# A routed feed-forward block on one core: routing steps of four links, search levels with fewer output tiles, tables loaded later

## The reference, cut to what matters

```python
h = rms_norm(x, gamma)                       # x: 2 x 2048 x 512
light = gelu(h @ w1_l + b1_l) @ w2_l + b2_l  # hidden 256, all tokens
s = einsum('bnd,d->bn', x, routing_token)
b = -relu(s)
for _ in range(50):                          # EPS = 0.1, K = 8
    a = EPS * log(K) - EPS * logsumexp((s + b) / EPS)   # over the 2048 tokens
    b = -relu(s + a)
scores = exp((s + a + b) / EPS)
sel = top_k(scores, 512)                     # per batch row
heavy = gelu(rms_norm(x[sel]) @ w1_h + b1_h) @ w2_h + b2_h   # hidden 2048
out = light; out[sel] += heavy * gain(scores)
```

## Time and profile before

| | us |
|---|---|
| median of 3 runs | 4053.99 (4047.73 to 4062.09) |
| the profiled execution, its own time | 4051.82 |
| its span | 4050.0 |
| PE busy in the span | 3908.2 (96%) |
| DVE busy | 2421.5 (60%) |
| ACT busy | 2004.7 (49%) |

### The profile page before, as it was taken

One profiled execution on the slowest core, in us unless ns is written; L12 is line 12 of the kernel. 1 busy time (PEld: TensorE's weight loads), 2 busy tenths in 40 slices (PEclk: granted clock), 3 DMA queues, 4 the chain that ended last, 5 costly groups with the idle time before them and its releaser, 6 DMA issues. The chain is left out here.

```text
span 4050.0 us, 58949 instructions
## 1 busy us (share of the span) xinstructions
PE 3908.2 (96%) x18715; PEld 2140.9 (53%) x18715; DVE 2421.5 (60%) x3329; ACT 2004.7 (49%) x3355; POOL 2684.8 (66%) x1402
## 2 busy tenths in 40 slices
PE   8999999999999999999999999999979999967899
PEld 7754444444444444444444444444448888854344
DVE  3466666666666666666666666666527777755400
ACT  3335555555555555555555555555434555533010
POOL 1138888888888888888888888888954444410010
PEclk9999999999999999999999999999989999989999
DMA  7632223222232342232222322223222333335510
GB/s 223 170 92 58 58 61 95 71 64 58 61 89 76 84 121 58 64 104 59 63 58 61 97 68 63 59 61 92 70 78 87 104 101 104 99 113 195 197 31 11
DMA packets 393979, 352.22 MB, mean 87 GB/s; under 512 B 192811, under 2 KB 267051, under 8 KB 392872
## 3 DMA queue, kind: packets, MB, share of 16 engines
q1 hardware_dynamic: 325800, 326.02, 28.0%
q10 hardware_dynamic: 66048, 16.78, 1.9%
q0 software_dynamic: 1920, 6.29, 0.5%
HBM read 142.63 MB, written 89.70 MB: 57 GB/s over the span
## 5 line engine op out<-in xcount | busy, mean ns | idle before, releaser
L328 POOL TENSOR_TENSOR acc<-acc,probs 128x1024 f32<-128x1024 f32 x894 | 2127.0, 2379 | 259.9 <-ACT probs L798 134.2
L928 DVE TENSOR_REDUCE maxes<-ps 128x1 f32<-128x1024 f32 x1024 | 1251.0, 1222 | 699.2 <-PE ps L579 694.7
L801 ACT ACTIVATE probs<-ps,far_bias 128x1024 f32<-128x1024 f32 (+7 forms) x1280 | 1021.9, 819 | 1017.2 <-DVE near_s L945 556.3
L614 PE MATMUL ps<-probs,v_head 128*64 128x512 f32 x4096 | 993.4, 606 | 2.0 <-ACT ctx_out L784 1.9
L579 PE MATMUL ps<-stacks 64*128 64x512 f32 x2048 | 748.4, 445 | 16.1 <-issue 7.3
L594 PE MATMUL ps<-stacks 64*128 64x512 f32 x1792 | 660.2, 448 | 0.0
L593 PE MATMUL ps<-stacks 128*128 128x512 f32 x2048 | 617.2, 418 | 1.2 <-ACT probs L798 1.2
L594 PEld LDWEIGHTS ps<-stacks 64*128 64x128 f32 x1792 | 275.9, 184 | 501.3 <-issue 329.4
L614 PEld LDWEIGHTS ps<-probs,v_head 128*64 128x64 f32 x4096 | 248.7, 136 | 483.3 <-issue 481.1
L593 PEld LDWEIGHTS ps<-stacks 128*128 128x128 f32 x2048 | 349.8, 188 | 216.9 <-issue 163.5
L945 DVE TENSOR_TENSOR near_s<-ps,near_bias 128x384 f32<-128x384 f32 (+2 forms) x576 | 284.7, 494 | 264.4 <-PE ps L594 241.4
(11 more groups left out here) (248 smaller groups left out, 4716.6 us busy)
## 6 DMA issues: line engine op xcount, KB each, us to landing
stacks<-c_k SPq DMA_DIRECT2D x128, 256.0 KB, 2.5
stacks<-c_q SPq DMA_DIRECT2D x128, 256.0 KB, 2.6
stacks<-c_d SPq DMA_DIRECT2D x256, 128.0 KB, 2.7
scr_v<-probs ACTq DMA_DIRECT2D x32, 512.0 KB, 4.1
stacks<-c_q SPq DMA_DIRECT2D x128, 128.0 KB, 2.7
v_head<-scr_v SPq DMA_DIRECT2D x32, 512.0 KB, 3.7
scr_ctx<-ctx_out SPq DMA_DIRECT2D x128, 128.0 KB, 2.3
both_ctx<-scr_ctx SPq DMA_DIRECT2D x32, 512.0 KB, 3.9
```

Of the source, the lines that this page charges most:

```text
L328: pool.tensor_tensor(acc[:, qb, :], acc[:, qb, :], pr, ALU.add).then_inc(s["summed"], 1)
L614: mm = pe.matmul(ps[64 * half:64 * half + 64, PV, :], v_head[:, side, kt, :], probs[:, st % PT_RING, half * 512:(half + 1) * 512], start=k ...
L801: ins = act.activation(probs[:, st % PT_RING, a:z], sc[:, a:z], ACT.Exp, bias=bias)
L928: dve.tensor_reduce(maxes[:, qt, pair:pair + 1], ps[:, bank:bank + 2, :], AX.XY, ALU.max).then_inc(s["max_done"], 1)
```

## The change

`hidden_of`: from step 6 on; what is left after step 49 (16 matmuls) is done after the loop. Scores are kept in units of EPS in a layout where partitions 0 to 63 hold batch row 0 and 64 to 127 row 1 (`s_half`, 128 x 2 x 16). A step is: DVE `arg` = min(ahead - log, 0); ACT exponential with the sum over its 32 columns in `sums`; PE sums over each half of the partitions with `own`; ACT logarithm read from PSUM. Beside that DVE keeps `lift` (the sum of the logarithms) and `ahead`. The wide table `s_max` is still used for the final scores and is loaded behind the fourth chunk. The other edits are order: w1, tables and `xb` behind the last chunk, gamma passes behind the GELUs, the row copy on DVE, two light tiles per level instead of four with three PSUM banks instead of four, the tables for the counts behind the search, and the last 12 tiles interleaved with the count matmuls of batch row 1.

```diff
-HIDDEN_FROM, HIDDEN_STEP = 2, 4
+HIDDEN_FROM, HIDDEN_STEP = 6, 4
+SPLIT_AT = 3
-LIGHT_IN_LEVEL = 4
+LIGHT_IN_LEVEL = 2
-LIGHT_IN_STEP = LIGHT_IN_LEVEL * LEVELS
+LIGHT_IN_STEP = LIGHT_IN_LEVEL * (LEVELS + 1)
...
 # SP
-            for b in range(NB):
-                sp.dma_start(s_max[:, b, 0:NT]..., scr["s"]...[b]).then_inc(s["s_in"], 16)
+            for b in range(NB):
+                for half in range(2):
+                    s_in(b, half)
...
-                if ch == 2:
-                    for j in range(4):
-                        xb_in(j)
                 if ch == 3:
-                    for dst, name in LOADS: ...
-                    for dst, name in ROWS: ...
+                    for b in range(NB):
+                        sp.dma_start(s_max[:, b, :]..., scr_s[b]).then_inc(s["s_max_in"], 16)
+            for dst, name in LOADS: ...
+            for j in range(4):
+                xb_in(j)
+            for dst, name in ROWS: ...
+            sp.dma_start(w1[:], io["w1h"]).then_inc(s["w1_in"], 16)
...
 # PE
             def light_mm(j):
-                if j >= 4:
-                    pe.wait_ge(s["light"], j - 3)
+                if j == 0:
+                    pe.wait_ge(s["hidden"], NCHUNK * LM)
+                if j >= 3:
+                    pe.wait_ge(s["light"], j - 2)
-                    mm = pe.matmul(ps[:, 4 + j % 4, :], ...)
+                    mm = pe.matmul(ps[:, 1 + j % 3, :], ...)
             for i in range(N_ITERS):
                 pe.wait_ge(s["ex"], i + 1)
-                pe.matmul(ps[:, 0, 0:NB * NT], ones[:], ex[:]...)
+                pe.matmul(ps[:, 0, 0:1], own[:], sums[:], start=True, stop=True).then_inc(s["mm"], 1)
                 for ch, m, at in hidden_of(i):
                     hidden_mm(ch, m, at)
+            pe.wait_ge(s["neg_a"], 1)
+            pe.matmul(ps[:, 0, 0:NB], ones[:], neg_a[:], start=True, stop=True).then_inc(s["neg_mm"], 1)
+            for ch, m, at in hidden_of(N_ITERS):
+                hidden_mm(ch, m, at)
             pe.wait_ge(s["score"], 1)
...
             mm.then_inc(s["bc"], 1)
+            light_mm(0)
+            light_mm(1)
...
-            for j in LIGHT_LAST:
+            for t, j in enumerate(LIGHT_LAST):
                 light_mm(j)
-            for t in range(NT - HM // 2):
                 hot_mm(1, t)
...
-                    if b == 0 and m < HM // 2:
-                        hot_mm(1, NT - HM // 2 + m)
+                    if b == 0 and m < NT - len(LIGHT_LAST):
+                        hot_mm(1, len(LIGHT_LAST) + m)
...
 # ACT
-                act.activation(ex[:], dif[:], ACT.Exp, scale=1.0 / ROUTE_EPS).then_inc(s["ex"], 1)
-                act.wait_ge(s["total"], i + 1)
-                act.activation(logs[:], total[:], ACT.Ln, scale=1.0 / K_ROUTE).then_inc(s["logs"], 1)
-                if i == 0:
+                act.activation(powers[:], arg[:], ACT.Exp, accum_out=sums[:]).then_inc(s["ex"], 1)
+                act.wait_ge(s["mm"], i + 1)
+                act.wait_ge(s["lift"], i + 1)
+                act.activation(log[:], ps[:, 0, 0:1], ACT.Ln, scale=1.0 / K_ROUTE).then_inc(s["logs"], 1)
+                if i == SPLIT_AT:
...
-            act.copy(rows[:], ps[:, 4:8, :]...).then_inc(s["bcr"], 1)
...
 # DVE
-                dve.tensor_tensor(low[:], s_max[:], neg_a[:]..., ALU.min)
-                dve.tensor_tensor(dif[:], low[:, :, 0:NT], spread(low[:, :, NT]), ALU.subtract)
+                dve.tensor_scalar(arg[:], ahead[:], log[:], 0.0, ALU.subtract, ALU.min).then_inc(s["dif"], 1)
+                if i:
+                    dve.tensor_tensor(lift[:], lift[:], log[:], ALU.add).then_inc(s["lift"], 1)
+                    dve.wait_ge(s["lift"], i + 1)
+                    dve.tensor_scalar(ahead[:], scaled[:], lift[:], None, ALU.subtract).then_inc(s["ahead"], 1)
-                dve.tensor_reduce(total[:], ps[:, 0, 0:NB * NT]...)
-                dve.scalar_tensor_tensor(neg_a[:], logs[:], ROUTE_EPS, low[:, :, NT], ALU.mult, ALU.add)
...
+            dve.tensor_tensor(low[:], s_max[:], spread(ps[:, 0, 0:NB]), ALU.subtract).then_inc(s["kept"], 1)
+            dve.tensor_copy(rows[:], ps[:, 4:8, :]...).then_inc(s["bcr"], 1)
...
-                if lv:
-                    for j in light_of_level(lv - 1):
-                        light_out(j)
+                for j in light_of_level(lv - 1):
+                    light_out(j)
...
+                    if b == 1 and t < len(LIGHT_LAST):
+                        light_out(LIGHT_LAST[t])
```

More of the change, by code:

```diff
@@ L1566 @@
 GAMMA_PIECES = HEAVY // 512
-GAMMA_FROM = 33
+HALF = P // NB
 def routed(nc, io, scr, out, index):
@@ L1588, in routed @@
         above = sb("above", [P, P])
-        s_max = sb("s_max", [P, NB, NT + 1])
-        top, top_row, top_diag = sb("top", [P, NB]), sb("top_row", [NB, 1]), sb("top_diag", [NB, NB])
-        low = sb("low", [P, NB, NT + 1])
+        s_max = sb("s_max", [P, NB, NT])
+        s_half = sb("s_half", [P, 2, NT])
+        scaled, ahead, arg, powers = (sb(n, [P, 2 * NT]) for n in ("scaled", "ahead", "arg", "powers"))
+        sums, log, lift = (sb(n, [P, 1]) for n in ("sums", "log", "lift"))
+        top, top_row, top_wide = sb("top", [P, 1]), sb("top_row", [1, NB]), sb("top_wide", [1, P])
+        low = sb("low", [P, NB, NT])
         dif, ex = sb("dif", [P, NB, NT]), sb("ex", [P, NB, NT])
-        total, logs = sb("total", [P, NB]), sb("logs", [P, NB])
         neg_a = sb("neg_a", [P, NB])
@@ L1623, in routed @@
         ps = c.enter_context(nc.psum_tensor("r_ps", [P, 8, 512], F32))
-        HOT, TURN = 0, 6
-        s = {n: sem(n) for n in """weights const zero s_in top_own top_turned top_row top_diag top_mm top gam low dif ex mm total logs neg_a arg kept sc1 sc score w
+        HOT, TURN, PAIRS = 0, 6, (4, 1)
+        s = {n: sem(n) for n in """weights w1_in const zero s_in s_max_in top_own top_turned top_row top_wide top_mm lift scaled ahead gam dif ex mm logs neg_a neg_mm arg kept sc1 sc score w
             bc bcr t1 cnt en en_mm f1 f2 base over mm1 r1 r2 r3s sel mm2 p1 p2 place hot hot_mm pairs pairs_tr parts4 gain edge_own edge_mm edge picked index
@@ L1632, in routed @@
         block = c.enter_context(nc.Block())
-        LOADS = [(w1, "w1h"), (gamma, "gamma_h"), (b1, "b1h"), (tokens, "tokens"), (steps, "steps"), (above, "above")]
+        LOADS = [(gamma, "gamma_h"), (b1, "b1h"), (tokens, "tokens"), (steps, "steps"), (above, "above")]
         ROWS = [(b2, "b2h"), (places, "places")]
@@ L1649, in _, with s_in @@
         def _(sp):
-            for b in range(NB):
[L1652 to L1655, removed]
+            def s_in(b, half):
+                sp.dma_start(s_half[HALF * b:HALF * b + HALF, half, :].rearrange("p (q t) -> p q t", t=TB),
+                             scr_s[b, HALF * half:HALF * half + HALF]).then_inc(s["s_in"], 16)
             def tokens_in(ch):
@@ L1875, in _ @@
             act.wait_ge(s["weights"], N_LOADS)
+            act.wait_ge(s["w1_in"], 16)
+            for k in range(KT):
+                for n in range(GAMMA_PIECES):
+                    piece = w1[:, k, n * 512:(n + 1) * 512]
+                    act.activation(piece, piece, ACT.Identity, scale=gamma[:, k:k + 1]).then_inc(s["gam"], 1)
             for b in range(NB):
@@ L1981, in _ @@
                 dve.wait_ge(s["base"], lv + 1)
-            for j in light_of_level(LEVELS - 1):
-                light_out(j)
             for b in range(NB):
@@ L1987, in _ @@
             ins.then_inc(s["edge_own"], 1)
+            dve.wait_ge(s["score"], 1)
+            dve.tensor_scalar(weight[:], score[:], -1.0, 1.0, ALU.mult, ALU.add).then_inc(s["w"], 1)
+            dve.wait_ge(s["w"], 1)
+            dve.tensor_tensor(gain[:], score[:], weight[:], ALU.add).then_inc(s["gain"], 1)
+            for b in range(NB):
+                dve.tensor_scalar(what[:, b, :, 0], tokens[:, 0, :], float(b * S), None, ALU.add)
+                dve.tensor_copy(what[:, b, :, 2], tokens[:, 1, :])
+            dve.wait_ge(s["gain"], 1)
+            dve.tensor_copy(what[:, :, :, 1], gain[:]).then_inc(s["gain"], 1)
+            dve.wait_ge(s["gain"], 2)
+            dve.tensor_tensor(what[:, :, :, 3], gain[:], what[:, :, :, 1].bitcast(F32), ALU.subtract).then_inc(s["gain"], 1)
+            for j in light_of_level(LEVELS - 1):
+                light_out(j)
             dve.wait_ge(s["edge_mm"], 1)
```

132 lines of the change are left out of this document (60 added, 72 removed).

## The result

The changed kernel takes 4024.68 us in the median (4021.22 to 4030.61, four runs), against 4052.23 for the kernel before, run beside it four times: a ratio of 0.9932, with a 95% interval of 0.9913 to 0.9951. It is faster, by 27.5 us in the medians, where the prediction said 4020. The profiled execution took 4021.22 us.

What follows compares the result with a forecast made beforehand. The prediction took a ring through ACT, PE and DVE, 1.84 us a step, as the bound. It summed 32.7 us by the last logarithm and 0.5 behind to 33.2, giving 4018.6, stated as 4020, range 4010 to 4036.

Steps and rivals of the forecast that it cites:

- signs of being wrong: Whole stage: PE token waits above 1 us, loop clock 0.5, first light output awaiting xb, heavy layer over 95 us after loop.
- First `arg`: Loop start: scores some 1.0 us later from four transfers, preparation 0.1 longer; first `arg` at 3620.3.
- Steps 0 to 5: Loop steps without hidden matmuls: 1.47 us each, 8.8 in all, plus 1.2 and 0.5 for weight splitting; 10.5 us.
- The step: Steps 6 to 49 of the loop: mean 1.30 us each, range 1.24 to 1.45, 57.2 us over 44 steps.
- The copy's own path: Every third loop step, DVE copies out a hidden block: next `arg` due 1.43 us after the last, other steps 1.25.
- Clock at the start: First two steps with hidden matmuls: still at the low clock, 2.14 us each, adding 1.7 us.
- Tokens: Loop's token loads: 8.3 us per pair, 0.5 us booked; as rival, 11 us loads become the bound, 4030, chance 0.12.
- Behind the loop: Last logarithm to heavy layer: 92.1 us against 91.7 before, 0.4 worse.
- The 0.9 for the heavy layer: Inside the heavy layer: four fewer count matmuls, 0.9 us better.
- Longer links: Rival in the loop: accumulator read exposed, logarithm link 0.30, or PE's queue delays sums; 1.5 us steps, 4029, chance 0.10.
- The tail: Rival in the ranking: each of the last 12 lights waits for its DVE output and count, +13.5 us, 4034, chance 0.05.
- The low clock: Rival in loop, possibly search: PE stays at 1.2 GHz, 2.14 us a step, 4062 or 4075, chance 0.03.

Runs made afterwards that it cites:

- e1: Changed kernel with a constant instead of the newest logarithm as the pointer operand of `arg` (routing not updated); 4024.02 us, one run.
- e3: Changed kernel with the exponential's sum over columns left out and `sums` set to 1 once; 4019.78 us, one run.
- e6: Changed kernel with each token chunk loaded in four pieces, each as soon as its buffer piece is free; 4025.28 us, ratio 0.9924 to the kernel before.
- e9: The changed kernel itself, run again; 4030.23 us, ratio 0.994 to the kernel before.
- e7: Changed kernel with three light tiles per search level instead of two; 4020.1 us, ratio 0.9915 to the kernel before.
- e4: Changed kernel with w1 and the tables loaded behind the fourth token chunk again, `xb` staying moved; 4040.88 us, ratio 0.9961 to the kernel before.

## Why the prediction was right, and where its terms were off

**Right:** faster, by the mechanism named. The DVE reduction is out of the ring, chunks are used in six steps, the clock is full from the third or fourth hidden step, the search is DVE's, the heavy layer starts earlier. The forecast of 4020 is 1.2 us from the profiled execution (4021.2) and 4.7 from the median, and that is partly luck: the sum was 6.3 us too good (33.2 for 26.9), and unchanged stages ahead were 3.7 us shorter in this execution; so the sum's own 4018.6 missed it by only 2.6. One of the forecast's own signs of being wrong did appear: PE rows that wait for tokens by more than 1 us (1.80).

Where the 6.3 us are, from the rows above:

- **First `arg`: 0.9.** It came 2.0 us later in the stage (6.64 for 4.67 us), forecast 1.1. The four score transfers take SP 0.61 to 0.68 us each, where the two of before took 0.39 and 0.50: DVE's first pass over the scores starts 1.7 us later in the stage (4.15 for 2.46 us), where 1.0 was booked. The preparation behind it is 0.3 longer, booked at 0.1:

```profile
L1663 SPq DMA_DIRECT2D r_s_half<-scr_s x4: 610/618/684, 3610.8 to 3612.8; - x4
```

- **Steps 0 to 5: 0.35.** 10.85 us for 10.5. The steps are 1.55, not 1.47; the split cost 1.55 us more, for 1.7 booked.
- **The step: 2.2.** 1.35 for 1.30, over 44 steps. Two links were too short in the forecast: `arg` to exponential was taken from a pass without a pointer operand (0.06, e1), and the logarithm was expected to leave sooner from PSUM; its own time did fall from 0.20 to 0.17 us, but the gap behind it is 0.11 instead of 0.03. The accumulator read was right (0.09, e3). The copy's own path was 1.37 us (it starts 0.76 behind `arg`, and the next `arg` follows it 0.61 later) for 1.43, and against a ring of 1.345 it costs 0.02 to 0.03 a time, where the forecast had it cost 0.18 against one of 1.25. That is why a ring 0.1 too short made the mean only 0.05 too short; in e1, with a ring of 1.28, every third step is 1.37 still.
- **Clock at the start: 1.0.** Three intervals at 2.13 to 2.24 us, where two were booked, and a first one of 1.55.
- **Tokens: 2.7.** 3.2 us of the loop for 0.5. The first refill was issued at 3639.77 and its chunk used at 3649.95: 10.2 us; later ones that PE waited for took 8.9, 8.6 and 9.4. The prediction's 8.3 is a misreading of its own row: 8.0 is the median of the pair's two landings, and half of the 0.6 us between their issues was added. A chunk is there only with the later of the two. First the pair of the earlier trace rows in the kernel before, then the first refill here, both from SP's line for the tokens:

```profile
DMA to landing us min/median/max: 7.0/8.0/9.0
...
DMA to landing us min/median/max: 6.4/8.0/9.5
```

  If the second transfer is the slower one, the pair of before took 0.6 + 9.0 = 9.6 us, and the refill here lands at 3640.4 + 9.5 = 3649.9, where PE starts. The other three fit in the same way (the slower landings are 8.3, 8.0 and 8.8). With D of 8.6 to 10.2 and C = 8.1 the prediction's own (C + D) / 2 gives 8.4 to 9.2 us. e6 took the waits away and the loop fell by 3.9.
- **Behind the loop: -0.75**, the only term better than forecast. 0.3 of it is there at the edge: levels of 4.45 us, since the two tile outputs hold DVE for 1.21 us (3711.60 to 3712.81), where 1.32 was booked. The rest lies between the edge and the heavy layer, 55.0 us for 55.4.

These are 0.9 + 0.35 + 2.2 + 1.0 + 2.7 - 0.75 = 6.4, with rounding the 6.3. The 0.9 for the heavy layer came as booked (26.0 us earlier at its start, 26.9 at the end of the span).

**The rivals.** *Tokens* is the one that partly came true: waits above 1 us, but 3.2 us in all and not 10, because the shorter chunks are late by a part of the period only. *Longer links* came true in small (1.35; not 1.5): of the two links it named, the one from the logarithm did reach 0.28 to 0.30, the accumulator read was as booked, and the one from `arg` to the exponential was not on its list. *The tail* gave nothing back. *The low clock* did not come in the changed kernel's two traces, but it is nearer than the 0.03 suggests. The first token wait is 1.80 us here and 2.04 in e9, and the clock stayed full behind both; behind 1.87 us in e7, whose loop is the same, it was 0.66, and behind 2.09 us in e1 0.56. So the length of the wait alone does not decide it, and these runs do not show what does. The Trainium skill, "TensorE: Matmul & The Clock Gate", section on HAM oscillation, says that short compute between DMA waits is throttled again at each tile. The traces agree behind the waits of 1.87, 2.09, 2.37 and 8.97 us (e7, e1, e3, e4), and do not for the 2.04 of e9 and the four waits of the changed kernel. Each time it cost two or three slow steps: the rival's price, the whole loop at the low clock, was not seen anywhere.

Not settled: why the unchanged stages ahead vary by 16 us between executions, and why ACT's logarithm from PSUM is seen later by DVE than the one from SBUF before it. A source in PSUM alone does not explain it: ACT's cast of 128x512 from PSUM ends at 3605.05 us in the changed kernel, and the DVE pass that waits for it starts at 3605.09. A logarithm of one column from SBUF was not tried in the new ring.

## What to carry to other kernels

When a ring of small operations is shortened, price the next resource from the release of its buffer to its use, with the last landing of all its transfers and not the median one, and release it in pieces: here quarters were worth 4.0 us, and without them a still shorter ring gained 1.4 us of the loop (e3) or lost 1.6 (e1). Measure a change in a late stage from that stage's own start, since stages that no one touched moved by more than half of the gain. When an engine becomes free in one stretch (PE in the search), look for work that waits behind a handshake further on: one light more per level was worth 5.6 us.

## What was not expected of the hardware

- A pointer operand on a DVE `tensor_scalar` of 128x32 costs 0.06 us: 0.24 us with it, 0.18 with a constant (e1).
- A token wait of 1.87 us was followed by a granted clock of 0.66 and two slow steps (e7), one of 2.09 us by 0.56 (e1), one of 2.04 us by none (e9). It cost e1 some 2.7 us.
- Two transfers of 1 MB issued 0.6 us apart landed 6.4 and 9.5 us behind their issues: the median of 8.0 says little on when the pair is there.
- The read of the accumulator, 0.19 us on the timeline, costs the reader 0.09 (e3).
- The same unchanged 3.6 ms of work ended between 3610.8 and 3626.6 us.
